# Router logits for four tiles at a time, low parts of a weight split on GpSimd, and one more tick of tile work in a short block

## The reference

```python
x = x + layernorm(attention(layernorm(x), Wq, bq, Wk, bk, Wv, bv))
h = layernorm(x)                               # h2 in the kernel, tile by tile
probs = softmax(h @ Wg)                        # Wg 512 x 8
eidx = argmax(probs); gate = probs[eidx]
pos = (cumsum(oh, axis=0) * oh).sum(-1) - 1    # oh: one-hot of eidx; place in the expert
keep = pos < 256                               # 256 rows for each of 8 experts
xd[eidx * 256 + pos] = h                       # dropped where not keep
oe = (silu(xd @ W1[e]) * (xd @ W3[e])) @ W2[e] # 8 experts, hidden size 704
out = oe[eidx * 256 + pos] * gate * keep
shared = silu(h @ sw1) * (h @ sw3) @ sw2
x = x + layernorm(out + shared)
```

## Time and profile before

| | us |
|---|---|
| median of 3 runs | 823.89 (823.04 to 825.83) |
| the profiled execution | 823.6 |
| its span, first to last instruction | 821.8 |
| TensorE busy | 777.9 (95%) |
| VectorE busy | 563.3 (69%) |
| ScalarE busy | 422.9 (51%) |
| GpSimd busy | 146.1 (18%) |
| chain that ended last | PE 65%, DVE 18%, DMA 5%, ACT 4%, issue 3% |
| mean granted TensorE clock | 0.989 of full speed |

### The profile page before, as it was taken

One profiled execution on the slowest core, in us unless ns is written; L12 is line 12 of the kernel. 1 busy time (PEld: TensorE's weight loads), 2 busy tenths in 40 slices (PEclk: granted clock), 3 DMA queues, 4 the chain that ended last, 5 costly groups with the idle time before them and its releaser, 6 DMA issues.

```text
span 821.8 us, 13879 instructions
## 1 busy us (share of the span) xinstructions
PE 777.9 (95%) x5060; PEld 651.3 (79%) x5060; DVE 563.3 (69%) x1196; ACT 422.9 (51%) x839; POOL 146.1 (18%) x229
## 2 busy tenths in 40 slices
PE   6999999999999999898999999999999999999994
PEld 4787887777777777676877887999999999887883
DVE  5764897578987566676588545466776666758666
ACT  5464352455656566666544244566675666723120
POOL 3300010410112014232344432000000000013122
PEclk9999999999999999999999999999999999999998
DMA  7789465975676788772339622676787776546444
GB/s 234 228 277 347 164 204 174 268 221 164 173 218 167 195 216 223 210 197 93 104 133 322 238 95 90 193 214 209 220 241 227 236 232 212 170 149 200 152 154 141
DMA packets 117492, 162.39 MB, mean 198 GB/s; under 512 B 17364, under 2 KB 65236, under 8 KB 117424
## 3 DMA queue, kind: packets, MB, share of 16 engines
q1 hardware_dynamic: 113840, 153.54, 61.8%
q0 software_dynamic: 3584, 7.97, 3.2%
HBM read 107.24 MB, written 55.05 MB: 197 GB/s over the span
## 4 chain that ended last, share of the span: by engine, by line
PE 65%; DVE 18%; DMA 5%; ACT 4%; issue 3%; POOL 1%; SPq 0%; POOLq 0%; DVEq 0%; ACTq 0%
PE bank L163 43%; PE wide L163 17%; DVE MX L160 4%; PE wide L167 3%; PE bank L167 2%; DVE SG L160 2%; DMA XX<-scr_xd 2%; DVE STC L281 1%; DMA scr_q<-hl 1%; DVE GC L153 1%; DMA scr_qtok<-H2A 1%; ACT PTG L145 1%; DMA H2A<-scr_oe,FG 1%; ACT PT L157 1%; DVE SIL L149 1%
## 5 line engine op out<-in xcount | busy, mean ns | idle before, releaser
L163 PE MATMUL wide<-W2H,HH 128*128 128x512 f32 x308 | 101.8, 396 | 0.5 <-ACT OUTR L145 0.5
L160 DVE TENSOR_REDUCE MX<-wide 128x1 f32<-128x192 f32 (+1 forms) x128 | 77.6, 647 | 20.9 <-PE wide L163 20.9
L157 ACT ACTIVATE PT<-bank 128x512 f32<-128x512 f32 x128 | 73.4, 593 | 29.1 <-PE bank L163 29.0
L157 ACT ACTIVATE SIL<-bank 128x256 f32<-128x256 f32 (+1 forms) x72 | 32.7, 454 | 98.1 <-PE bank L163 97.8
L149 DVE TENSOR_TENSOR SIL<-bank,SIL 128x256 f32<-128x256 f32 (+1 forms) x72 | 36.9, 512 | 64.0 <-ACT SIL L157 63.3
L163 PE MATMUL bank<-XT,W13H 128*128 128x256 f32 (+1 forms) x336 | 76.6, 322 | 0.0
L145 ACT ACTIVATE HH<-SIL 128x256 fp32r<-128x256 f32 (+1 forms) x72 | 35.2, 489 | 66.6 <-DVE SIL L149 66.6
L163 PEld LDWEIGHTS wide<-W2H,HH 128*128 128x128 f32 x308 | 58.6, 190 | 13.3 <-ACT OUTR L145 1.3
L149 DVE TENSOR_TENSOR HH<-SIL,HH 128x256 fp32r<-128x256 f32 (+1 forms) x72 | 37.0, 514 | 45.9 <-ACT HH L145 37.7
L163 PE MATMUL wide<-W2L,HH 128*128 128x512 f32 x168 | 66.5, 396 | 0.8 <-DVE W2L L149 0.7
L163 PEld LDWEIGHTS bank<-XT,W13H 128*128 128x128 f32 x336 | 55.0, 188 | 4.7
(11 more groups left out here) (256 smaller groups left out, 2010.4 us busy)
## 6 DMA issues: line engine op xcount, KB each, us to landing
R<-in_L_ffn_W_dram SPq DMA_DIRECT2D x48, 512.0 KB, 5.6
scr_q<-hl SPq DMA_DIRECT2D x16, 512.0 KB, 4.3
scr_k<-hl SPq DMA_DIRECT2D x16, 512.0 KB, 4.1
R<-in_L_ffn_sw_dram SPq DMA_DIRECT2D x12, 512.0 KB, 5.4
QSe<-scr_q SPq DMA_DIRECT2D x36, 128.0 KB, 3.7
KSe<-scr_k SPq DMA_DIRECT2D x36, 128.0 KB, 3.7
R<-_attn_hidden_states_dram SPq DMA_DIRECT2D x16, 256.0 KB, 3.9
scr_qtok<-H2A SPq DMA_DIRECT2D x16, 256.0 KB, 3.8
```

The lines of the kernel that those rows point to most:

```text
L157: return do("act", lambda g: g.activation(dst, src, fn, **kw), after)
L160: return do("dve", lambda g: g.tensor_reduce(dst, src, AXX, op), after)
L163: return do("pe", lambda g: g.matmul(ps, a, b, start=start, stop=stop, skip_group_check=True), after, mark=mark)
```

## The change

logits_group makes the logits of four tiles at once for groups 0 and 1: Wg is the weight that is held (16 columns), and the 512 tokens of XT stream, eight matmuls that leave the sums as 16 x 512 in a bank of UP. ScalarE copies them to a tile of XL, and logits_fold turns them back by four fp32 matmuls with fold, a 16 x 8 matrix of two identities that adds the high and the low half on the way. split_2 makes the low parts of W2 on GpSimd for job 0 and on VectorE for the others. q=0 gets a tick after m=5, so all later ticks stand one place earlier, and q=1 has none after m=5 but route_place(3). Within a tick h_turn now comes before h_logits, and the count of groups 0 and 1 right behind h_turn; the counts are at ticks 8, 13, 16, 20 and the placements at 9, 14, 18 and after m=5 of q=1.

```diff
--- before.py
+++ after.py
@@ -178,6 +178,7 @@
         onesb = sb(top, "onesb", [P, P], BF16)
         wgs = sb(top, "wgs", [P, 4, E])
         wghl = sb(top, "wghl", [P, 4, 2, E], F32R)
+        fold = sb(top, "fold", [2 * E, E])
         wt8 = sb(top, "wt8", [P, E])
         e256 = sb(top, "e256", [P, E])
         mhalf = sb(top, "mhalf", [P, 1])
@@ -679,6 +680,7 @@
                                 split_w(1, c)
                         if n == 1 and c == 3 and g4 == 0:
                             m_wg.extend(split(wghl[:, :, 0, :], wghl[:, :, 1, :], wgs[:, :, :], "dve", [m_bias]))
+                            m_wg.append(tt(fold[:, :], ident[0:2 * E, 0:E], ident[0:2 * E, E:2 * E], ALU.add, [m_id]))
                             stores.append(dma("sp", zs, lambda g: g.dma_start(
                                 xdd.rearrange("(i p) d -> p i d", p=P),
                                 zt[:, :].unsqueeze(1).broadcast_to([P, 16, D])), [k0]))
@@ -1323,8 +1325,10 @@
             free2 = [[] for _ in range(6)]
             w2m = [[] for _ in range(6)]
 
-            def split_2(j, m, e_hi):
-                w2m[m] = split(W2H[:, m, :], W2L[:, m, :], r2[:, m, :], e_hi, [m2[j, m // 2]] + free2[m] + begun + fence_ct)
+            def split_2(j, m, e_lo):
+                after = [m2[j, m // 2]] + free2[m] + begun + fence_ct
+                a = copy("act", W2H[:, m, :], r2[:, m, :], after)
+                w2m[m] = [a, tt(W2L[:, m, :], r2[:, m, :], f(W2H[:, m, :]), ALU.subtract, after + [a], e=e_lo)]
                 busy2[m // 2] += w2m[m]
 
             hfree = [[] for _ in range(6)]
@@ -1399,37 +1403,47 @@
             route = dict(cum=m_cum)
             scat_slots = [slot() for _ in range(4)]
             scat = []
+            def logits_group(g4):
+
+                ui, ps, fr = UP.take()
+                li, lt, lf = XL.take()
+                x_ = xt[g4]
+                for l in range(2):
+                    for k in range(4):
+                        m_l = mm(ps[0:2 * E, :], wghl[:, k, :, :].rearrange("p l e -> p (l e)"),
+                                 x_["b"][l][:, k, :], k + l == 0, k + l == 4, x_["ready"] + m_wg + fr, mark=(k == 3 and l == 1))
+                XT.busy[x_["i"]].append(m_l)
+                m_c = copy("act", lt[0:2 * E, :, :].rearrange("p k t -> p (k t)"), ps[0:2 * E, :], [m_l] + lf)
+                UP.busy[ui].append(m_c)
+                route["lt"] = (li, lt, m_c)
+
+            def logits_fold():
+
+                li, lt, m_c = route["lt"]
+                route["mi"], route["mb"], fr = MSC.take()
+                for j in range(4):
+                    m_l = mm(route["mb"][:, j * 16:j * 16 + E], lt[0:2 * E, j, :], fold[:, :], True, True,
+                             [m_c] + m_wg + fr, mark=(j == 3))
+                XL.busy[li].append(m_l)
+                route["m_l"] = m_l
+
             def h_logits(t):
 
-                g4, j = divmod(t, 4)
+                j = t % 4
                 d = hs[t]
                 if j == 0:
                     route["mi"], route["mb"], route["mfree"] = MSC.take()
-                mb, dst = route["mb"], d["dst"]
-                if g4 < 2:
-                    col = d["col"]
-                    for k in range(4):
-                        for l in range(2):
-                            m_l = mm(mb[:, j * 16:(j + 1) * 16].rearrange("p (l e) -> p l e", l=2),
-                                     dst[l][:, k, col:col + P], wghl[:, k, :, :], k == 0 and l == 0,
-                                     k == 3 and l == 1, d["s"] + m_wg + route["mfree"], mark=(k == 3 and l == 1))
-                    XT.busy[xt[g4]["i"]].append(m_l)
-                else:
-                    for k in range(4):
-                        m_l = mm(mb[:, j * 16:j * 16 + E], dst[:, k, :], wgs[:, k, :], k == 0, k == 3,
-                                 d["s"] + m_wg + route["mfree"], mark=(k == 3))
-                    XL.busy[d["li"]].append(m_l)
+                for k in range(4):
+                    m_l = mm(route["mb"][:, j * 16:j * 16 + E], d["dst"][:, k, :], wgs[:, k, :], k == 0, k == 3,
+                             d["s"] + m_wg + route["mfree"], mark=(k == 3))
+                XL.busy[d["li"]].append(m_l)
                 route["m_l"] = m_l
 
             def route_count(g4):
 
                 mb, m_l, m_cum = route["mb"], route["m_l"], route["cum"]
                 lg = mb[:, 0:64].rearrange("p (j l e) -> p j l e", j=4, l=2)
-                if g4 < 2:
-                    a = copy("act", LG[:, 0, :, :], lg[:, :, 1, :], [m_l, m_cum])
-                    a = tt(LG[:, 1, :, :], lg[:, :, 0, :], LG[:, 0, :, :], ALU.add, [a])
-                else:
-                    a = copy("dve", LG[:, 1, :, :], lg[:, :, 0, :], [m_l, m_cum])
+                a = copy("dve", LG[:, 1, :, :], lg[:, :, 0, :], [m_l, m_cum])
                 L = LG[:, 1, :, :]
 
                 def bc(v):
@@ -1560,22 +1574,26 @@
                 finals.append(m_o)
 
             tick = [7]
+            COUNT_AT, PLACE_AT = {8: 0, 13: 1, 16: 2, 20: 3}, {9: 0, 14: 1, 18: 2}
 
             def work():
 
                 n = tick[0]
                 tick[0] += 1
                 if n == 7:
-                    h_logits(0)
-                    h_logits(1)
-                for back, fn in ((5, h_logits), (4, h_turn), (3, h_h2), (2, h_mean2), (1, h_x1), (0, h_mean)):
+                    logits_group(0)
+                if n in (8, 13):
+                    logits_fold()
+                if n == 12:
+                    logits_group(1)
+                for back, fn in ((4, h_turn), (5, h_logits), (3, h_h2), (2, h_mean2), (1, h_x1), (0, h_mean)):
                     t = n - back
-                    if 4 <= t < 16 or 0 <= t < 4 and fn is h_logits:
+                    if (8 if fn is h_logits else 4) <= t < 16:
                         fn(t)
-                        if fn is h_logits and t % 4 == 3:
-                            route_count(t // 4)
-                if n % 4 == 1 and 9 <= n <= 21:
-                    route_place(n // 4 - 2)
+                    if n in COUNT_AT and fn is (h_turn if n < 16 else h_logits):
+                        route_count(COUNT_AT[n])
+                if n in PLACE_AT:
+                    route_place(PLACE_AT[n])
 
 
             work()
@@ -1611,7 +1629,7 @@
                     if last and m % 2 == 1:
                         next_13(m // 2)
                     if first:
-                        split_2(job, m, "act")
+                        split_2(job, m, "pool" if job == 0 else "dve")
                     if q == 0 and m < 4:
                         split_13(0, m + 2, "act")
                         if m < 3:
@@ -1619,8 +1637,10 @@
                         else:
                             for g3 in range(3):
                                 load_13(1, g3)
-                    if q == 1 or q == 0 and m < 5:
+                    if m < 5 and q < 2 or q == 0:
                         work()
+                    if q == 1 and m == 5:
+                        route_place(3)
                     if job == 9:
                         t0 = 4 * (g - 2)
                         if 0 <= m - 2 < 4:
```

## The result

The changed kernel takes 831.8 us (median of 4 runs, 828.8 to 835.0) against 823.5 us (822.2 to 825.8) for the one before. The ratio is 1.0109 [1.0079, 1.0139]. The forecast was 829.0 us and slower: the direction is right, and the size too small. The medians differ by 8.4 us where the forecast had 5.1 to 5.8, and the time lies 0.8 us outside the range.

A forecast was written before the change was run, and what follows sets the result against it. TensorE is busy nearly throughout but waits on VectorE, which sets the pace in q=0. TensorE 7.4 us late (5.9 + 1.5 slow clock) less 1.6 at the end of q=1 gives 5.8 on 823.6: 829.4, stated as 829.0; range 821.2 to 831.0.

The forecast's parts named there:

- First wait, 412.6: Before tile 5's transposes in q=0: TensorE's idle time grows to 2.7 us, gain to there only 0.45, slow stretch stays.
- W2L on GpSimd: Job 0's W2 subtraction takes 1.28 us on GpSimd, and VectorE's instruction with two SBUF inputs is held until it ends.
- Rival A: GpSimd's subtractions don't slow VectorE: 824.2 to 825.7 us, half a hold about 827; chance 0.20 with its half.
- rival B: Faster: the clock stays up at m=1's end because W2L off VectorE brings L942 early; 821.3 or 820.6 us; chance 0.16.
- The added tick: After m=5 of q=0: tile 8's logits wait for route_count(1) to read their bank; TensorE idles 4.1 us.
- Rival C: The bank's wait is hidden because VectorE is ahead at m=5, tile 10 waits 2.2 us instead: 825.6 us; chance 0.12.
- +1.5 slow clock: Behind the bank wait in q=0: 1.5 us added for a low clock, as both earlier gaps were followed by one.
- End of q=1: TensorE no longer waits for OHB and CUMB; the scatter and XX loads limit the gain to 1.6 of 3.4 us.
- rival D: At the XX loads TensorE idles up to 1.8 us; a clock fall in job 1 costs 1.5 more: 830.5 us; chance 0.10.
- The work that the grouped logits save: Logits of groups 0 and 1: TensorE's matmul work falls by 1.85 us, 0.84 of it at 397 to 400.

The follow-up runs named there:

- a2: The changed kernel with the ticks back where they were (none after m=5 of q=0, one after m=5 of q=1); ratio to the kernel before 1.0035.
- b2: The changed kernel with W2L of job 0 on VectorE and the old ticks, leaving grouped logits, fold and order within a tick; ratio to before 0.9998.
- a1: The changed kernel with the low parts of W2 of job 0 back on VectorE, all else as changed; ratio to the kernel before 1.0063.
- b1: The kernel before with only the low parts of W2 of job 0 moved to GpSimd; ratio to the kernel before 1.0032.
- a4: The changed kernel with W2L of job 0 on VectorE and tile 8's logits at the head of tick 14; ratio to the kernel before 1.0009.
- b3: The kernel before with only the ticks moved: one after m=5 of q=0, none after m=5 of q=1; ratio to before 1.0020.
- a3: The changed kernel with only the logits of tile 8 moved from tick 13 to the head of tick 14; ratio to the kernel before 1.0080.
- c1: The kernel before with group 3's count halfway through m=4 of q=1, counts issued behind h_h2 and placement 0 one tick later; ratio to before 1.0071.
- b4: The kernel before with tick 20 (tile 15's logits, group 3's count) between the two banks of m=4 of q=1, tick 21 after m=4; ratio to before 0.9960.

## Why the prediction was right in kind and too small in size

Times on the axis of the old trace (after + 1.80).

| step | forecast | measured |
|---|---|---|
| transposes of tile 5 | 414.5 | 414.36 |
| transposes of tile 7 | 430.25 | 430.25 |
| logits of group 1 | 436.3 | 437.93 |
| logits of tile 8 start | 446.95 | 448.70 |
| tick 14 ends, next W2H | 454.8 | 458.67 |
| from placement 3 to job 1 | 19.85 | 18.53 |

- **First wait, 412.6: right.** TensorE idle 2.7 forecast; measured 2.17, or 2.3 with the drain of the matmul before. The slow stretch stayed, the gain to there is 0.6 us where 0.45 was forecast.
- **W2L on GpSimd: right that VectorE is held to GpSimd's end, too narrow in what is held.** Rival A (no hold) is out by the pairs of W13L at 2.05, rival B with it. CX at 2.15 instead of 0.54 is a tensor-scalar instruction with one tensor input, and I had counted only those with two. Its 1.6 us is what group 1 is late (437.93 against 436.3), and in sum most of tile 8's 1.75. The sum hides some luck: the 1.0, 0.8 and 0.3 us of hold forecast for HH's low part of m=3 and the L942 of steps 3 and 4 came as 0 (HH took 0.69), 0 and 1.1 (L944 at 440.50), with 0.7 on a W13L (1.41 at 433.98) and 0.3 of idle time before it. The Trainium skill (SBUF — State Buffer, SBUF: two separate sides) says that a VectorE instruction in a 2-port mode and one of GpSimd exclude each other for a whole instruction, and (DVE: opcode table, instruction layouts, handler registers and perf-mode slots, Perf-mode slots) that a one-source instruction gets such a mode at fp32 too. By these pages CX can be among those held, and the trace agrees: it ends 0.29 us after the W2L beside it, though it began 0.53 us ahead of it, during the scatter. Which mode it ran in, and what the scatter did to it, no run here shows.
- **The added tick: right in place and releaser.** TensorE was said to idle 4.1; it's 3.6 named, between those two instructions. Rival C (hidden) is out.
- **The step that failed is the size of "+1.5 slow clock" behind the bank wait.** I took the 1.5 from a gap of 1.25 and one of 1.44 us. With one of 3.6 the clock was at 0.50 for 6.6 us of work, and at 0.90 for 3.5 more: 3.3 + 0.35 instead of 1.5. It accounts for the 2.1 us between the forecast's 7.85 and the measured 9.97 from tile 8's logits to the end of tick 14.
- **End of q=1: right in direction.** OHB and CUMB wait no more, but 21.44 - 18.53 = 2.9 us were given back, not 1.6. 1.7 of the 21.44 are the slow stretch of that one execution: in a2 and b2, with the same waits and no low clock there, it's 19.9. The two XX loads were issued in 0.79 us instead of 1.83, and TensorE waited just 0.26 for them: rival D's gap didn't come.

```profile
517.85 0.97 POOL L1490 DMA_INDIRECT scr_xd<-GC,FSI  x1 [0.31 <-issue]
```

```profile
520.21 0.79 SPq L1525 DMA_DIRECT2D XX<-scr_xd  x2
```

(GpSimd's last scatter and SyncE's loads behind it, after.) In sum: +1.75 for the hold of CX, +2.1 for the clock, -1.3 at the end, on a forecast of 5.8: 8.35, measured 8.1. The work that the grouped logits save was put 0.3 too high (1.5 measured in b2), which didn't matter, as it turned into waiting. The experiments bear out the parts that they could take away: W2L (a1, b1), the tick and its bank wait (a2, a4, b3), and no gain from less matmul work (b2). The slow stretch's length was read, not varied by itself; a1 has 6.5 us of it behind a wait of 2.7, so it isn't this one execution, but what sets the length stays open. The length of the wait alone doesn't: 6.8 us at the low clock follow a wait of 2.3 in a3 and of 1.9 in c1, none follow one of 2.35 in b2 and of 1.9 in b3.

## What to carry to other kernels

Matmul work saved beside a VectorE-paced stretch turns into waiting; look for the instruction that TensorE will wait for next before counting the saving (b2: 1.5 us less work, 3.1 more of idle time). Where matmuls need in the same step what an in-order engine has yet to do, be it a result or a bank to be read, put other work between the two on both engines. b4 does so for the count and its placement, halfway through a run of matmuls and ahead of VectorE's long instructions, and a3 and a4 put the bank's next writer a tick later. A subtraction of 0.6 us moved to GpSimd took 1.3 there and added 0.7 to 1.4 to the VectorE instruction beside it; and a step moved later (c1's placement) takes the buffers with it that its DMAs still read.

## What the runs showed that I hadn't expected

- A one-input CX instruction of VectorE was held for 2.15 us across a scatter and a subtraction of GpSimd, in two kernels (after and b1).
- The same waits had a low clock behind them in one execution and not in another: those for OHB and CUMB in before, but not in a2, b1 and b2. A difference of 1.7 us between two profiles can be this alone, as in b4.
- The tick cost 0.2% alone and 0.7% with the grouped logits, whose order put the reader of the bank and its next writer into that tick; W2L on GpSimd cost 0.3 to 0.5% with each.
